# The end of a fused layer pair rewritten in the 65 dimensions of the last state and 32 of the memory

## The chip, the cores and the metric

One core of one Trainium2 chip. The metric is the device time of one execution in microseconds (us), lower is better; several executions are timed and their median is taken. Engines: TensorE (PE, with its weight loads PEld), VectorE (DVE), ScalarE (ACT), GpSimd (POOL), SyncE (SP, which issues all the DMAs here).

## What is computed

Input `x` is 8 sequences of 256 tokens, 2048 tokens of 512 values, float32. Cut to what matters:

```python
# first half: x1 = x + LN(attn(LN(x)))
h = LN(x) @ Win.T + bin                        # 64 dimensions
for layer in range(4):
    y = sconv(silu(LN(h)))                     # diagonal complex recurrence along the 256 tokens
    h = h + y * scl
    h = h + silu(LN(h) @ W1.T + b1) @ W2.T + b2   # 64 -> 256 -> 64
x1 = x + LN(LN(h) @ Wout.T + bout)             # 64 -> 512
# second half: out = x1 + LN(ffn(LN(x1)))
xn = LN(x1)
q = xn @ Wq.T                                  # 64 dimensions
scores = (q @ Wr.T) @ (keys @ Wr.T).T / sqrt(48) + log_rel     # 128 slots
top 8 of the scores; attn = q @ keys.T / sqrt(64) + log_rel over those 8; w = softmax
aux = (w @ values) @ Wvd.T @ Wvu.T             # 32 dimensions between
u = f(var(xn), mean over all tokens of log1p(var), gelu(xn @ Wu1.T + bu1) @ Wu2.T)
gate = sigmoid(...), zero below 0.05
out = x1 + LN(xn + gate * aux)
```

## The kernel before

The 2048 tokens are 16 tiles of 128 (TILES), in 4 groups of 4 tiles (GROUPS, GT). A unit u is one group in one layer, so there are 16 units. Every engine has its instructions written out by hand, in its own order, and waits on semaphores.

**Setup and start.** SP issues all input loads in one row: weights, then for each group the transposed input `XT` and `X` (1 MB each). PE's `first_h` (L1031) multiplies a group of `XT` by the input weights into the group's own PSUM bank (banks 2 to 5), where the state h of the group stays through all layers. ACT's `input_squares` (L397) sums the squares of x for the input norm, POOL's `input_rstd` (L312) makes 1/sqrt of it, and DVE's `first_h` (L716) scales h. DVE builds the tables of the recurrence. `keep_busy` (L1043) has PE multiply ones by ones into an unused part of a bank: 10 times before `turn1(0)`, 6 times before `turn1(1)` and `turn1(2)`.

**The steps.** 20 steps (STEPS, `step` on each engine) form a pipeline in which a unit passes: square on ACT (`square`, L449), sum on DVE (`sum_squares`, L729), power -0.5 on POOL (`norm`, L328), scaling on DVE (`scale_twice`, L735), transposes on PE (`turn1`, L1057), silu on ACT (`silu1`, L454), multiplication, scan and multiplication on DVE (L751, L760, L766), `mix_in` on PE (L1070), a second norm, `turn2` (L1082), `z_out` on ACT, `hidden` on PE (L1095), two silus on ACT (L476) and one step later `project` on PE (L1104, L1110). In step s, PE does turn1(s), project(s-3), turn2(s-2), mix_in(s-1), hidden(s-2), and in steps 4 to 9 one piece of `setup_late` (L1006), which multiplies the weights of the end together. In the same step ACT does square(s+1) after silu1(s); the unit s+1 is ready for it once project(s-3) is done. DVE does `score_rows` (L697) in step 6. PE's, ACT's and DVE's queues are in order: what is behind a wait stands.

**The first half's end.** Steps 16 to 19 hand over the last normed state as `ZL` (64 rows and a row of ones). For every tile PE multiplies it by `WO`, 512 wide (`output`, L1140); ACT squares and sums it (L505), POOL makes 1/sqrt (`pair_rstd`, L340), DVE adds it to X (`first_result`, L809), takes statistics (L814), POOL makes the next 1/sqrt, DVE normalises into `XN` (L822).

**The second half.** PE transposes XN in four pieces (`turn_xn`, L1151), ACT copies them out (L510), and PE makes 384 columns in four pieces of 128 rows each (`scores`, L1164): 128 routing scores, 128 attention scores, 128 inputs of the gelu. ACT does the gelu (L516); DVE finds the top 8 and masks the others (`select_pair`, L830), and takes the largest (`pair_max`). These run two pairs behind `output` on the same engines. Then the gate is worked out in small steps on DVE, ACT takes exponentials of a pair (`exps`, L535), PE transposes them (`turn_e`, L1195), ACT copies them out (`e_out`, L540), PE multiplies by the 512-wide `V2` (`memory`, L1207), DVE adds the result to XN (`mix`, L966), ACT sums the squares (L546), POOL makes 1/sqrt, and DVE (12 tiles, `finish`, L972) or POOL (4 tiles, L370 and L373) writes the output tile; SP stores a pair of tiles at a time (L282).

## Time and profile before

| | |
|---|---|
| median of 3 runs | 251.32 us (251.24 to 251.65) |
| the profiled execution | 250.35 us |
| its span, first to last instruction | 248.5 us |
| PE busy | 196.7 us, 79% |
| DVE busy | 181.2 us, 73% |
| ACT busy | 128.3 us, 52% |
| POOL busy | 89.4 us, 36% |
| mean granted clock of PE | 0.952 of full speed |

The first `turn1` starts at 21.89 us, that of step 16 at 126.89, that of step 19 at 141.91; the last output tile is finished at 245.3. A busy share is an average over stages with different limits; the rows below are therefore taken by stage. A matmul of float32 shows as two records, a transpose as one. The records of a run of matmuls overlap, so the pace of a run is its length over its records.

### The profile page before, as it was taken

The numbers are of one execution on the slowest core, as the hardware profiler recorded it, in microseconds if no ns is written. First come the engines' busy times: TensorE is split into PE (matmuls) and PEld (weight loads), VectorE is DVE, ScalarE is ACT, GpSimd is POOL, SyncE is SP. The second block draws the span as 40 slices with busy tenths as digits, with TensorE's granted clock in tenths as the row PEclk, the third lists the DMA queues.
The fourth block names the chain that finished last, engine by engine and source line by source line (L and its number), as shares of the span: only waits on it lengthen the run. The fifth ranks groups of instructions, "written<-read, shape, count | busy, mean of one in ns | idle before, by whom it ended". The sixth has DMA issues, their size and how long they took to land.

```text
span 248.5 us, 3501 instructions
## 1 busy us (share of the span) xinstructions
PE 196.7 (79%) x1148; PEld 145.2 (58%) x1148; DVE 181.2 (73%) x507; ACT 128.3 (52%) x306; POOL 89.4 (36%) x118
## 2 busy tenths in 40 slices
PE   2699596389959998878888759999999999399600
PEld 2699495377848787767776525565556555143200
DVE  7799895557784777767663174977797775889993
ACT  4328728246543667575565644343243329587640
POOL 8213333433342443533334332121212110048772
PEclk9999989799997999999999999999999999979965
DMA  5999900000000000000000000000000000003346
GB/s 197 425 415 419 258 9 4 0 0 1 3 0 0 3 0 0 4 0 0 3 0 3 0 0 1 1 3 0 0 0 0 0 3 1 0 0 120 135 169 253
DMA packets 5407, 15.09 MB, mean 61 GB/s; under 512 B 909, under 2 KB 1773, under 8 KB 4366
## 3 DMA queue, kind: packets, MB, share of 16 engines
q1 hardware_dynamic: 5390, 14.88, 16.2%
q8 instruction: 9, 0.15, 0.2%
q14 instruction: 8, 0.07, 0.1%
HBM read 10.68 MB, written 4.19 MB: 60 GB/s over the span
## 4 chain that ended last, share of the span: by engine, by line
PE 49%; DVE 25%; POOL 10%; ACT 9%; issue 4%; POOLq 0%; DVEq 0%; ACTq 0%
PE bank L1164 15%; PE bank L1110 12%; POOL RS L328 8%; PE bank L1140 5%; PE bank L1057 4%; DVE Z L735 3%; DVE SS L729 3%; PE bank L1207 3%; PE bank L1070 2%; ACT SQ L449 2%; PE bank L1151 2%; DVE XT L966 2%; DVE X L972 2%; PE bank L1038 2%; PE bank L1095 1%
## 5 line engine op out<-in xcount | busy, mean ns | idle before, releaser
L328 POOL TENSOR_TENSOR RS<-SS,nhalf 128x4 f32<-128x4 f32 x36 | 43.1, 1209 | 72.0 <-DVE SS L729 71.8
L1164 PE MATMUL bank<-SW_,Y 128*128 128x384 f32 x128 | 43.9, 485 | 0.0
L729 DVE TENSOR_REDUCE SS<-SQ 128x4 f32<-128x260 f32 x36 | 15.1, 423 | 26.1 <-ACT SQ L449 25.0
L1164 PEld LDWEIGHTS bank<-SW_,Y 128*128 128x128 f32 x128 | 23.9, 190 | 17.0 <-issue 4.2
L1110 PE MATMUL bank<-ffst,HD 128*128 128x128 f32 x256 | 33.5, 287 | 0.0
L1110 PEld LDWEIGHTS bank<-ffst,HD 128*128 128x128 f32 x256 | 32.4, 205 | 0.3
L449 ACT ACTIVATE SQ<-bank 128x256 f32<-128x256 f32 x36 | 13.8, 383 | 29.4 <-PE bank L1110 18.1
L476 ACT ACTIVATE HD<-bank,b1r 128x512 f32<-128x512 f32 x32 | 20.3, 684 | 12.1 <-PE bank L1095 12.1
L1057 PE MATMUL bank<-ident,Z 128*128 128x128 f32 x64 | 11.5, 306 | 18.0 <-DVE Z L735 17.9
L1057 PEld LDWEIGHTS bank<-ident,Z 128*128 128x128 f32 x64 | 7.3, 151 | 23.7 <-DVE Z L735 23.7
L809 DVE SCALAR_TENSOR_TENSOR X<-bank,OR,X 128x512 f32<-128x512 f32 x16 | 11.3, 746 | 12.3 <-POOL OR L346 12.2
L760 DVE TENSOR_TENSOR_SCAN V<-cvst,U 128x514 f32<-128x514 f32 x16 | 19.5, 1219 | 0.0
L1095 PE MATMUL bank<-Z,w1r 64*128 64x256 f32 x128 | 18.1, 402 | 1.6 <-ACT Z L470 1.6
L1038 PE MATMUL bank<-wcc,XT 128*128 128x128 f32 x128 | 17.3, 300 | 2.2 <-DVE wcc L633 2.2
L516 ACT ACTIVATE V<-bank 128x128 f32<-128x128 f32 x16 | 4.3, 277 | 28.4 <-PE bank L1164 28.4
L1038 PEld LDWEIGHTS bank<-wcc,XT 128*128 128x128 f32 x128 | 16.9, 217 | 2.5 <-issue 2.4
L1070 PE MATMUL bank<-cvst,U 128*128 128x128 f32 x128 | 17.9, 285 | 0.1
L1140 PE MATMUL bank<-WO,ZL 128*128 128x512 f32 x32 | 16.2, 597 | 1.6 <-DVE X L809 1.6
L1207 PE MATMUL bank<-V,U 128*128 128x512 f32 x32 | 16.8, 649 | 0.8 <-ACT U L540 0.7
L454 ACT ACTIVATE Y<-bank,cvst 128x512 f32<-128x512 f32 x16 | 12.4, 777 | 9.6 <-PE bank L1057 9.6
L1070 PEld LDWEIGHTS bank<-cvst,U 128*128 128x128 f32 x128 | 16.4, 201 | 0.3 <-DVE U L766 0.3
L735 DVE TENSOR_TENSOR Z<-bank,RS 128x512 f32<-128x512 f32 x16 | 11.1, 691 | 7.0 <-POOL RS L328 6.9
(219 smaller groups left out, 376.1 us busy)
## 6 DMA issues: line engine op xcount, KB each, us to landing
XT<-in_xT SPq DMA_DIRECT2D x4, 1024.0 KB, 11.4
X<-in_x SPq DMA_DIRECT2D x4, 1024.0 KB, 14.1
out<-X SPq DMA_DIRECT2D x8, 512.0 KB, 2.8
w1r<-in_w1d SPq DMA_DIRECT2D x1, 516.0 KB, 11.6
lt<-in_late SPq DMA_DIRECT2D x1, 385.5 KB, 19.3
w2r<-in_w2n SPq DMA_DIRECT2D x1, 256.0 KB, 7.1
SW_<-in_wu SPq DMA_DIRECT2D x1, 256.0 KB
c<-in_c SPq DMA_DIRECT2D x1, 172.5 KB, 21.8
```

Of the source, the lines that this page charges most:

```text
L328: pool.tensor_tensor(RS[:, g, :], SS[:, g, :], nhalf[:, :], ALU.pow).then_inc(done, 1)
L476: act.activation(HD[:, u % 2, a, :].rearrange("p (h n) -> p h n", h=2), FB[a], ACT.Silu, bias=b1r[:, 2 * L + a:2 * L + a + 1]).then_inc(g2, 1)
L729: dve.tensor_reduce(SS[:, g, :], SQ[:, g, :, :], AX.X, ALU.add).then_inc(done, 1)
L760: dve.tensor_tensor_scan(V[:, g, :], cvst[:, L, DC0:DC0 + UC], U[:, g, :], 0.0, ALU.mult, ALU.add).then_inc(v1, 1)
L1038: last = pe.matmul(HK[g][:, j * P:(j + 1) * P], XT[:, g, c, j * P:(j + 1) * P], wcc[:, c, :], start=(j == 0 and c == 0), stop=(c == VC - 1 ...
L1057: last = pe.transpose(T1B[:, j * P:(j + 1) * P], Z[:, g, j * P:(j + 1) * P], ident[:, :])
L1070: last = pe.matmul(HK[g][:, j * P:(j + 1) * P], U[:, g, j * P:(j + 1) * P], cvst[:, L, MX0:MX0 + P], start=False, stop=True, skip_group_ch ...
L1095: last = pe.matmul(FB[a][:, h, :], w1r[h * DIM:(h + 1) * DIM, L * DFF + a * P:L * DFF + (a + 1) * P], Z2[h * DIM:(h + 1) * DIM, g, :], sta ...
L1110: last = pe.matmul(HK[g][:, j * P:(j + 1) * P], HD[:, u % 2, a, at:at + P], ffst[:, L, a * P:(a + 1) * P], start=False, stop=True, skip_gr ...
L1140: pe.matmul(OB[t % 2][:, :], ZL[:, t // GT, (t % GT) * P:(t % GT + 1) * P], WO[:, :], start=True, stop=True).then_inc(o_mm, 1)
L1164: last = pe.matmul(SBK[t % 4][:, 0:SW], XNT[:, t % 4, c * P:(c + 1) * P], SW_[:, c, :], start=False, stop=(c == VC - 1))
L1207: pe.matmul(MB[t % 4][:, :], ET[:, t // 2 % 2, (t % 2) * P:(t % 2 + 1) * P], V2[:, :], start=True, stop=True).then_inc(aux_mm, 1)
```

## The change

1. x is multiplied, tile by tile, by a stacked matrix M of 289 columns (65 of the output weights with their bias, 128 of Wu1, 64 of Wq, 32 of Wvu), centred over its 512 rows. `project_x` on PE: four pieces of 128 rows, into bank 1, which `turn2` uses too; `x_out` on ACT copies the 289 columns out. Tiles are placed in steps by `XSTEP`.
2. At the start four small matmuls (`mix_columns`) and four of 289 columns (`column_sums`) stand on PE before `first_h(1)`; ACT copies both out before its step 0; POOL centres M (`centre_m`). `first_h(3)` moves from step 1 to step 0. `keep_busy` goes. M is loaded before the second group's XT.
3. The last state stays token-major in `F`, and transposed in `ZL`. The variance of the 512-wide result comes from a Gram matrix: `gram` on PE (four matmuls of 65 columns) and DVE, `cross` on POOL, `rho` and `first_rstd` on POOL.
4. `mixed` on PE (224 columns, 65 rows deep, one per tile) and `project` on DVE add the state's part to x's part; `unscore` on DVE, `scaled` and `gelu` on ACT, `turn_q` on PE, `qt_out` on ACT follow, and `scores` has 256 columns and 64 rows of depth.
5. In the last loop the memory is 32 wide (`memory`, two matmuls of 64 columns), `dots` on DVE and a chain of some ten small operations on POOL give the last norm, `factors` on DVE writes the factors into F, and one 512-wide matmul a tile (`output`) with one DVE operation (`finish`) makes the output tile. POOL no longer writes output tiles.
6. `setup_late` has five other pieces, in steps 4 to 8; `score_rows` is 256 wide (before: 384); `output_sums` and `setup_last` go.

The core of the diff:

```diff
+        XSTEP = {1: (0, 1), 2: (2, 3), 3: (4,), 9: (5,), 11: (6,), 13: (7,), 15: (8,), 16: (9,), 17: (10, 11),
+                 18: (12, 13), 19: (14, 15)}
+        SELS = PAIRS
+        BATCHES = ((0, 4), (4, 8), (8, 12), (12, 14), (14, 16))
+        LAST = [e // 2 - 1 for _, e in BATCHES]
+        MIXLAG = 3
+        FIN = {4: (0,), 5: (1,), 6: (2,), 7: (3,), 8: (4,), 9: (5, 6), 10: (7,)}
...
 ACT
+            def x_out(t):
+                act.wait_ge(xa_mm, t + 1)
+                act.activation(XA[:, t, :], LB[:, 0:MW], ACT.Copy).then_inc(xa_read, 1)
...
                 if 0 <= s - LATE0 < LATES:
                     setup_late(s - LATE0)
+                for t in XSTEP.get(s, ()):
+                    x_out(t)
...
+            for k in range(SELS + MIXLAG):
+                if k < SELS:
+                    exps(k)
                     e_out(k)
+                    y_out(k)
+                if k == 1:
+                    act.wait_ge(sig_in, 1)
...
+                for p in FIN.get(k, ()):
+                    f_out(p)
...
 DVE
+                g = s - UNITS - 1
+                if g >= 1:
+                    first_variance(g - 1)
+                if g >= 0:
+                    gram(g)
+                if g >= 1:
+                    project(g - 1)
...
+            def project(p):
+                for t in (2 * p, 2 * p + 1):
+                    dve.wait_ge(am_mm, 2 * p + 2)
...
+            def finish(t):
+                dve.wait_ge(o_mm, t + 1)
+                dve.scalar_tensor_tensor(out=X[:, t, :], in0=X[:, t, :], scalar=GX[:, 4, t:t + 1], in1=OB[t % 2][:, :],
+                                         op0=ALU.mult, op1=ALU.add).then_inc(out_ready, 1)
...
+            for k in range(SELS + MIXLAG):
+                if k < SELS:
+                    select(k)
+                for i in range(len(BATCHES)):
+                    if LAST[i] + MIXLAG == k:
+                        factors(i)
+                if k == 0:
+                    for p in range(5):
+                        learned(p)
+                if k == 1:
+                    for p in range(5, PAIRS):
+                        learned(p)
+                    gate_learned()
                     gate_sum()
+                if k == 2:
                     gate_mean()
+                    gate_level()
+                if 0 <= k - 1 < SELS:
+                    dots(k - 1)
+                if k == 2:
+                    gate()
+                for p in FIN.get(k, ()):
+                    finish(2 * p)
+                    finish(2 * p + 1)
...
 PE
+            def project_x(t, s):
+                pe.wait_ge(m_done, VC)
+                pe.wait_ge(cs_read, 1)
+                if t >= 1:
+                    pe.wait_ge(xa_read, t)
...
+                for c in range(VC):
+                    last = pe.matmul(LB[:, 0:MW], XT[:, g, c, j * P:(j + 1) * P], M[:, c, :], start=(c == 0),
+                                     stop=(c == VC - 1))
...
-                if u < 3:
-                    keep_busy(10 if u == 0 else 6)
...
-                if s + 2 < GROUPS:
-                    first_h(s + 2)
+                if s == 0:
+                    first_h(2)
+                    first_h(3)
                 if ffn:
                     hidden(s - 2)
                 if 0 <= s - LATE0 < LATES:
                     setup_late(s - LATE0)
+                for t in XSTEP.get(s, ()):
+                    project_x(t, s)
...
+            for s in range(STEPS):
                 step(s)
+                if s >= UNITS:
+                    gram(s - UNITS)
+                if s >= UNITS + 2:
+                    mixed(s - UNITS - 2)
...
+            mixed(2)
+            for p in range(PAIRS):
+                if p + 3 < PAIRS:
+                    mixed(p + 3)
+                turn_q(p)
+            scores(0)
+            scores(1)
+            for k in range(SELS + MIXLAG):
+                if k < SELS:
                     turn_e(k)
+                    memory(k)
+                    if k + 2 < SELS:
+                        scores(k + 2)
+                if k == 1:
+                    mean_sum()
+                for p in FIN.get(k, ()):
+                    turn_f(p, min(k + 1, SELS))
+                    output(2 * p)
+                    output(2 * p + 1)
```

`turn_e(k)` waits for the exponentials of pair k (`exps(k)` on ACT), which wait for `select(k)` on DVE. `turn_f(p, n)` transposes F of two tiles into the bank that `turn_e` uses, and waits for the n-th `e_out` and for `factors`; `f_out` on ACT copies it out. `mixed(p)` for odd p waits until `project(p-1)` is done.

## Rows read from the trace of the kernel before

**Rows 1.** Busy time by stage: PE, PEld, DVE, ACT, POOL (instructions), clock, DMA share, GB/s.
```profile
139.20:211.30 72.10, 67.23 (x253) 38.93 (x251) 51.08 (x180) 32.13 (x80) 15.85 (x33) 1.00 0.00 1
211.30:245.30 34.00, 18.29 (x44) 7.19 (x44) 31.49 (x70) 19.39 (x68) 18.83 (x24) 0.85 0.28 104
245.30:248.50 3.20, 0.00 (x0) 0.00 (x0) 0.03 (x1) 0.00 (x0) 0.00 (x0) 0.50 0.56 210
```

**Rows 2.** Chain that ended last: start, us, what.
```profile
98.38 0.66 PE bank L1057 x4
...
126.89 0.63 PE bank L1059 x4
...
131.89 0.63 PE bank L1059 x4
...
174.40 2.58 PE bank L1164 x8
```

**Rows 3.** Timeline of step 11 and the start of step 12: start, us, engine, line.
```profile
98.98 1.95 PE L1110 MATMUL bank<-ffst,HD 128*128 128x128 f32 x16
...
101.97 1.13 PE L1095 MATMUL bank<-Z,w1r 64*128 64x256 f32 x8
...
104.05 0.66 PE L1057 MATMUL bank<-ident,Z 128*128 128x128 f32 x4 [0.95 <-DVE Z L735]
```

**Rows 4.** Timeline, steps 2 and 3.
```profile
34.95 0.38 ACT L449 ACTIVATE SQ<-bank 128x256 f32<-128x256 f32 x1 [1.18 <-DVE bank L722]
...
44.17 0.38 ACT L449 ACTIVATE SQ<-bank 128x256 f32<-128x256 f32 x1
...
47.73 1.12 PE L1057 MATMUL bank<-ident,Z 128*128 128x128 f32 x4 [4.76 <-DVE Z L735]
```

**Rows 5.** Timeline, step 7, behind the pause that score_rows leaves.
```profile
74.01 0.70 PE L1057 MATMUL bank<-ident,Z 128*128 128x128 f32 x4 [2.80 <-DVE Z L735]
...
74.72 3.47 PE L1110 MATMUL bank<-ffst,HD 128*128 128x128 f32 x16
```

**Rows 6.** Timeline, from the last selects to the memory's matmuls.
```profile
207.25 0.49 DVE L834 MAX8 M<-bank 128x8 f32<-128x128 f32 x2
...
209.57 0.42 DVE L854 TENSOR_REDUCE NMX<-cvst 128x2 f32<-128x256 f32 x1
...
214.22 0.17 DVE L908 TENSOR_SCALAR GA<-GA 128x16 f32<-128x16 f32 x1
...
215.87 0.17 DVE L916 TENSOR_SCALAR GA<-GA 128x16 f32<-128x16 f32 x1
...
216.20 0.39 ACT L535 ACTIVATE U<-cvst,NMX 128x128 f32<-128x128 f32 x1
...
217.11 0.44 PE L1195 MATMUL bank<-ident,U 128*128 128x128 f32 x2 [3.44 <-ACT U L535]
...
217.59 0.38 ACT L540 ACTIVATE U<-bank 128x256 f32<-128x256 f32 x1 [0.53 <-PE bank L1195]
...
223.11 1.88 PE L1207 MATMUL bank<-V,U 128*128 128x512 f32 x4
```

**Rows 7.** Lines: what, shape, count, busy us, mean ns, idle before.
```profile
L809 DVE SCALAR_TENSOR_TENSOR X<-bank,OR,X 128x512 f32<-128x512 f32 x16 | 11.3, 746 | 12.3 <-POOL OR L346 12.2
L972 DVE SCALAR_TENSOR_TENSOR X<-XT,ZR,X 128x512 f32<-128x512 f32 x12 | 11.2, 970 | 0.6 <-POOL ZR L346 0.6
L827 DVE SCALAR_TENSOR_TENSOR V<-V,lt 128x128 f32<-128x128 f32 x16 | 3.9, 282 | 0.0
L743 DVE TENSOR_TENSOR Z<-bank,RS 128x256 f32<-128x256 f32 x20 | 8.1, 407 | 3.3 <-POOL RS L328 3.3
```

**Rows 8.** Windows of a microsecond, columns as in rows 1.
```profile
215.00:216.00 1.00, 0.00 (x0) 0.00 (x0) 0.86 (x5) 0.00 (x0) 0.00 (x0) 1.00 0.00 0
...
218.00:219.00 1.00, 1.00 (x2) 0.46 (x2) 0.97 (x4) 0.79 (x3) 0.00 (x0) 0.50 0.00 0
...
221.00:222.00 1.00, 1.00 (x3) 0.42 (x3) 0.97 (x3) 0.98 (x4) 0.92 (x2) 0.87 0.00 0
```

More of the change, by code:

```diff
@@ new lines, in _ @@
+            for s in range(STEPS):
+                if s == 0:
+                    mix_rows()
+                    column_means()
+                step(s)
+                if s == 0:
+                    ffn_out()
+            for p in range(PAIRS):
+                scaled(2 * p)
+                scaled(2 * p + 1)
+                gelu(p)
+                if p >= 1:
+                    qt_out(p - 1)
+            qt_out(PAIRS - 1)
+            act.wait_ge(ln_in, 1)
+            act.activation(GA[:, 3, :], GA[:, 2, :], ACT.Ln).then_inc(ln_out, 1)
@@ new lines, in _ @@
+            first_variance(2)
+            gram(3)
+            unscore(0)
+            project(2)
+            unscore(1)
+            project(3)
+            unscore(2)
+            project(4)
+            unscore(3)
+            first_variance(3)
+            project(5)
+            unscore(4)
+            gate_variance()
+            project(6)
+            unscore(5)
+            project(7)
+            unscore(6)
+            unscore(7)
+            for k in range(SELS + MIXLAG):
[11 more added lines that the diff above has]
+                    gate_learned()
@@ L1004, in setup_ffn, with mix_columns, column_sums @@
                 last.then_inc(w2_mm, 1)
+            def mix_columns():
+                pe.wait_ge(s_m, 32)
+                pe.wait_ge(lt_ready, 3)
+                for c in range(VC):
+                    last = pe.matmul(LB[:, c * ZD:(c + 1) * ZD], WOR[:, c * P:(c + 1) * P], LT[:, :], start=True,
+                                     stop=True)
+                last.then_inc(bp_mm, 1)
+            def column_sums():
+                pe.wait_ge(bp_read, 1)
+                for c in range(VC):
+                    last = pe.matmul(LB[:, 0:MW], ones[:, :], M[:, c, :], start=(c == 0), stop=(c == VC - 1))
+                last.then_inc(cs_mm, 1)
@@ L1013, in setup_late @@
+                vals = ltc("vals").rearrange("p (c n) -> p c n", c=VC)
+                wvd = ltc("wvd").rearrange("p (c n) -> p c n", c=VC)
+                if i == 0:
+                    for c in range(VC):
+                        last = pe.matmul(LB[0:VB, NSLOT:2 * NSLOT], wvd[:, c, :], vals[:, c, :], start=(c == 0),
+                                         stop=(c == VC - 1))
                 if i == 1:
-                    pe.wait_ge(s_late, 48)
-                    vals = ltc("vals").rearrange("p (c n) -> p c n", c=VC)
@@ L1029, in setup_late @@
+                    last = pe.matmul(LB[:, NSLOT:NSLOT + VB], vpT[:, :], G2[:, :], start=True, stop=True)
+                if i == 4:
+                    pe.wait_ge(mf_done, 1)
+                    for c in range(VC):
+                        last = pe.transpose(LB[:, c * P:(c + 1) * P], MF[:, c, :], ident[:, :])
                 last.then_inc(late_mm, 1)
@@ L1041, in first_h @@
                 last.then_inc(h0_mm, 1)
-            def keep_busy(n):
-                for _ in range(n):
-                    pe.matmul(T2B[:, HW:HW + P], ones[:, :], ones[:, :], start=True, stop=True)
             def turn1(u):
                 g = u % GROUPS
-                if u < 3:
-                    keep_busy(10 if u == 0 else 6)
                 pe.wait_ge(z1, u + 1)
@@ new lines, in gram, with mixed @@
+            def gram(g):
+                if g == 0:
+                    pe.wait_ge(zm_eps, 1)
+                pe.wait_ge(y1, UNITS + g + 1)
+                pe.wait_ge(z1, UNITS + g + 1)
+                for j in range(GT):
+                    last = pe.matmul(GB[g][:, j * ZD:(j + 1) * ZD], ZL[:, g, j * P:(j + 1) * P], ZM[:, 0:ZD], start=True,
+                                     stop=True)
+                last.then_inc(gr_mm, 1)
+            def mixed(p):
+                g = p // 2
+                pe.wait_ge(gr_prod, g + 1)
+                if p % 2:
+                    pe.wait_ge(t_done, 2 * p)
+                for t in (2 * p, 2 * p + 1):
+                    pe.matmul(AB[g][:, t % 2, 0:AW], ZL[:, g, (t % GT) * P:(t % GT + 1) * P], ZM[:, ZD:MW], start=True,
+                              stop=True).then_inc(am_mm, 1)
@@ new lines, in turn_f, with output @@
+            def turn_f(k, after):
+                i = min(i for i in range(len(BATCHES)) if 2 * k + 2 <= BATCHES[i][1])
+                pe.wait_ge(f_done, i + 1)
+                pe.wait_ge(et_ready, after)
+                if k >= 1:
+                    pe.wait_ge(ft_ready, k)
+                for j in range(2):
+                    last = pe.transpose(EB[:, j * P:(j + 1) * P], F[:, 2 * k + j, :], ident[:, :])
+                last.then_inc(f_tr, 1)
+            def output(t):
+                pe.wait_ge(ft_ready, t // 2 + 1)
+                if t >= 2:
+                    pe.wait_ge(out_ready, t - 1)
+                else:
+                    pe.wait_ge(qt_done, PAIRS)
+                    pe.wait_ge(gsum_read, 1)
+                pe.matmul(OB[t % 2][:, :], FT[:, t // 2 % 2, (t % 2) * P:(t % 2 + 1) * P], FM[:, :], start=True,
+                          stop=True).then_inc(o_mm, 1)
```

726 lines of the change are left out of this document (369 added, 357 removed).

## The prediction, written before the changed kernel was run

> **What bounds the kernel now.** I read the busy times by stage first, then the chain that ended last, then timelines of single steps. Three stages have three limits. In the end of the first half and the scoring (139.2 to 211.3 us) PE is busy 67 of 72 us [rows 1]; the chain there is matmul behind matmul, with 2.58 us for the 384 columns of each tile [rows 2]. From 211.3 to 245.3 DVE is busy 31.5 of 34 us [rows 1]. Before them, a step (from 98.38 to 104.05, 5.67 us [rows 2, 3]) is bound by a loop: transposes and `project` on PE, square, sum, power and scaling on the other engines. PE is done with `hidden` at 103.10 and waits 0.95 us for the scaled group [rows 3]. So PE has about one free microsecond a step, and none in the end. The change takes PE and DVE work out of the end and puts a part of it into the steps.
>
> **What goes.** From turn1(16) at 126.89 [rows 2] to the end at 248.5 are 121.6 us; this stretch is replaced whole, so I lay out the new one and don't subtract.
>
> **The price of `project_x`.** 8 records of 384 columns take 2.58 us, so 8 of 289 columns take 2.58 x 289/384 = 1.94 us at the high clock. The copy `x_out` has 289 columns, a little over the 256 of `e_out`, 0.38 [rows 6]; I take 0.42. Bank 1 is single, so two tiles in one step cost 2 x 1.94 + 0.5.
>
> **Start: +7.8.** The extra matmuls before `first_h(1)` (1.94 for the column sums, about 0.6 for the small ones) push square(1) back by about 1.5, which `first_h(3)`, now earlier, gives back. Then comes the term that counts. In steps 1 and 2 `x_out` stands at the end of ACT's step, ahead of square(2) and square(3). PE starts tile 0 after mix_in(0), near 33.6; tile 1 is copied out near 38.8, so square(2), before at 34.95 [rows 4], starts there. In step 2 the same again: turn1(2) near 42, mix_in and `hidden` to 46, tiles 2 and 3 to 51.1. square(3), before at 44.17 [rows 4], comes at 51.1: +6.9. Sum, power and turn1(3) follow it as before, so turn1(3) moves from 47.73 [rows 4] to 54.6. Tile 4 in step 3 takes 1.94 of PE against 1.0 free: +0.9. Bounds of this part: +4 if PE's short waits stay at the high clock and the copies overlap, +9 if not.
>
> **Steps 4 to 8: -1.9.** The new `setup_late` pieces are about as long as the old, +0.3. `score_rows` has 256 columns for 384, -0.5. And step 6 now has 1.94 us of matmuls (289 columns, four pieces) in the pause in which PE waited 2.80 us; behind that pause 16 records took 3.47 us [rows 5] in place of 1.95 [rows 3], at half clock. I take the pause as filled and the fall as gone, -1.7; bound 0.
>
> **Steps 9 to 15: +4.0.** Four tiles, one in a step, each 1.94 + 0.1 against 0.95 free [rows 3]: +1.1 each. `setup_last`, which delayed step 13, goes: -0.4. turn1(16) so comes at 126.9 + 7.8 - 1.9 + 4.0 = 136.8.
>
> **Steps 16 to 18: 26.2.** Step 16 is bound by PE: 4.65 of old work, 1.94, and `gram` (four matmuls of 65 columns, near 0.7): 7.3. Step 17 (4.5 of old work, two tiles 4.4, gram 0.6): 9.6. Step 18: 2.3 + 4.4 + 0.6 + `mixed` 0.75 = 8.0, and then `project(0)` on DVE (two of 224 columns, by 407 ns for 256 [rows 7]) stands ahead of the scaling that turn1(19) needs: 9.3. turn1(19) at 163.0; before 15.0 after turn1(16).
>
> **To the first select: 20.** PE reaches `mixed(1)` 6.2 us into step 19. Behind it DVE has 7 pairs of `project` (0.7), 8 of `unscore` (0.5), a gram product and sum (1.15), two variances (1.2), `gate_variance` (1.9) and short waits for `mixed` (0.7): 19 to 20. First select at 183.0.
>
> **Turns 0 to 3 of the last loop: 18.5, bound by DVE.** A select took 2.74 from 207.25 to 209.99 [rows 6], with two `learned` (0.28 long, a little over 0.2 apart [rows 7]) and one mask operation (about as long) that go: 2.05. Four of them 8.2; 8 pairs of `learned` 3.6; the gate's small operations at 0.21 each (8 from 214.22 to 216.04 [rows 6]) 4.1 in all; three `dots` at 0.7; 0.6 of waits. Turn 4 starts at 201.5.
>
> **Turns 4 to 7: 33.2, bound by a chain.** Here is the step that decides. In PE's queue turn_f, and with it the output matmuls, stand behind `turn_e(k)`, which waits for the exponentials of pair k, which wait for select(k); and in DVE's queue `finish` stands ahead of select(k+1). So nothing of turn k+1 overlaps turn k. Its length: select 2.05; exponentials 0.05 + 0.86 (216.20 to 217.06); turn_e 0.05 + 0.44; e_out 0.04 + 0.38 [rows 6]; memory 0.4; scores, bias rows and two 64-row matmuls of 256 columns, 0.8; turn_f 0.45; f_out 0.43; two output matmuls 0.1 + 1.88 [rows 6]; the last `finish` 0.05 + 0.75 [rows 7]. Sum 8.7; without scores in turns 6 and 7, 7.9. Two of each: 33.2. DVE works 4.8 of each.
>
> `finish` replaces L972, mean 970 ns, but reads PSUM as L809 does, mean 746 ns [rows 7]; I take 0.75, since the operands are L809's. The Trainium skill (GPSIMD Engine Reference, the table of its specifications) says that GpSimd contends with VectorE instructions with two SBUF inputs. `finish` has one, so by it 0.75 holds even beside GpSimd; at L972's 0.97 the sum would be about 1.5 us longer, as only the last of a pair is on the path.
>
> **Turns 8 to 10: 14.1, and 3.2 behind.** Turn 8 is factors, turn_f, f_out, two outputs, finish: 4.5. The last three pairs overlap on PE and DVE: 9.6. From the last finish to the end 3.2, as now [rows 1]. At the high clock the sum is 201.5 + 33.2 + 14.1 + 3.2 = 252.0.
>
> **The clock: +5.** When PE stood idle for 3.4 us up to 217.11 [rows 6], the granted clock was still 1.00 in the window from 215, fell to 0.50 as work came back, and rose in the window from 221 [rows 8]: from 2.4 to 1.2 GHz for almost 4 us. In each of turns 4 to 7 PE stands 3.8 us (0.8 + 2.05 + 0.96). I let turn_e, memory, scores and turn_f run at half clock: +1.35 with scores, +1.1 without, 5 in all. Bounds: 0, or +3.5 a turn if the outputs run slow too, 14. The Trainium skill (TensorE: Matmul & The Clock Gate, the section on the HAM clock gate) says that the ramp costs under 1% of a typical span. That would be under 2.5 us here and give a span of at most 254.5; step 7 alone lost 1.5 [rows 3, 5], so I keep 5.
>
> **Sum.** Span 257.0. The profiled execution took 1.85 us more than its span (250.35 for 248.5), so 258.9, against 250.35: +8.5. The median of the runs lies 1.0 above the profiled execution, inside the error of this sum. I forecast 259.
>
> **The rivals.**
> Slower, high clock kept in turns 4 to 7: 252.0 + 1.9 = 253.9. For it: the memory stage kept 0.85 of the clock though PE was busy 18 of 34 us [rows 1]; against: pauses of 4.76, 2.80 and 3.44 us each ended in slow records [rows 4, 5, 8]. Chance 0.2.
> Slower, low clock throughout the last loop: +9 on the forecast at most, some 266. Chance 0.1.
> Faster: the last loop is bound by DVE, not by the chain. Place: turns 4 to 7. If they took DVE's 4.8 each, 33.2 would become 19 and the clock term go: 252.0 - 14 + 1.9 = 240. It decides against me as soon as a turn takes under 7.8 us with the slow clock counted (8.5 us in four turns). For it: DVE filled 31.5 of 34 us in the same place before [rows 1]; against: the order of the queues. Together with a start at its lower bound this is the faster side. Chance 0.26.
> No change: the 41 us (16 x 2.58 [rows 2]) of PE's scoring and what is added cancel; a band of 1 us in a spread of 20. Chance 0.04.
> The forecast itself: 0.4.
>
> Faster, same and slower mean more or less than 0.2%, about what a measurement of this kernel can tell from no change: 0.26, 0.04, 0.70. The range leaves out a tenth on either side: 243 holds most of the faster case, 267 the low clock.
>
> **What would show it.** turn1(3) near 54.6 with ACT's square(3) behind `x_out`, turn1(16) near 137, turn1(19) near 163, first select near 183. In turns 4 to 7 starts of select 8 to 10 us apart, DVE idle ahead of `finish` for PE, the clock falling in each. Wrong if selects are 5 us apart, or if turn1(16) comes before 132.

## The result and the profile after

The changed kernel takes 281.93 us (median of 4 runs, 279.75 to 282.54) against 251.45 (251.24 to 251.65) for the kernel before: ratio 1.1197, interval 1.1133 to 1.126, **slower by 12%**. The forecast was 259, from 243 to 267: right in the sign, wrong by 23 us in the size. The profiled execution took 279.75 us with a span of 277.9. Executions of one and the same kernel lie some microseconds apart, the longer ones with the lower granted clock (the changed kernel from 279.75 us at 0.840 to 282.54 at 0.824, e7_start_lag_gatevar below from 244.88 at 0.909 to 251.28 at 0.876), so medians are compared with medians, and lengths of stages are read from the profiled executions.

The place of each term of the sum, forecast and found (starts in us of the span; the length in brackets where that is what was forecast):

| place | forecast | found | miss of the term |
|---|---|---|---|
| turn1(3) | 54.6 | 55.34 | |
| turn1(16) | 136.8 | 138.85 | +2.05 |
| turn1(19) | 163.0 (26.2 behind it) | 166.86 (28.0) | +1.8 |
| first select | 183.0 (20) | 195.24 (28.4) | +8.4 |
| turn 4 | 201.5 (18.5) | 213.79 (18.55) | 0 |
| end of turn 7 | 33.2, and 5 for the clock | 259.56 (45.8) | +7.6 |
| last finish ends | 14.1 | 274.66 (15.1) | +1.0 |
| span | 257.0 | 277.9 | +20.9 |

Two terms hold 16 of the 21 us. Busy time by stage, cut at those places (columns as in [rows 1]):

```profile
21.90:55.30 33.40, 23.02 (x134) 18.06 (x134) 20.69 (x48) 18.70 (x44) 12.77 (x12) 0.92 0.25 99
55.30:138.90 83.60, 79.44 (x590) 68.34 (x591) 56.49 (x100) 46.64 (x93) 31.15 (x28) 0.97 0.00 1
138.90:166.90 28.00, 24.66 (x161) 20.35 (x159) 7.21 (x20) 9.22 (x19) 8.96 (x10) 1.00 0.00 1
166.90:195.20 28.30, 19.45 (x71) 14.09 (x72) 15.02 (x51) 12.92 (x37) 7.73 (x12) 0.67 0.00 0
195.20:213.80 18.60, 12.17 (x46) 6.58 (x44) 15.36 (x96) 6.61 (x26) 1.69 (x6) 0.50 0.01 1
213.80:259.60 45.80, 29.62 (x72) 13.70 (x72) 16.25 (x62) 8.44 (x33) 9.58 (x39) 0.59 0.09 35
259.60:277.90 18.30, 10.64 (x24) 4.02 (x24) 7.67 (x17) 1.53 (x4) 2.56 (x11) 0.91 0.39 145
```

In the fourth and sixth no engine is full: PE 19.45 of 28.3 and 29.62 of 45.8, VectorE 15 and 16. Such a stage is bound by a chain that passes from engine to engine. The stage that I took for VectorE's and that mostly was (the fifth, 15.36 of 18.6) came out as forecast, in part by luck, as told further down.

The same cut for the whole of the replaced part, before and after, is the case in two lines. The kernel before, from its turn1(16), then the changed kernel from its own:

```profile
126.90:248.50 121.60, 96.39 (x385) 55.69 (x385) 87.13 (x258) 58.83 (x160) 38.15 (x61) 0.94 0.09 35
```
```profile
138.90:277.90 139.00, 96.55 (x370) 58.73 (x368) 61.52 (x243) 38.73 (x116) 30.51 (x77) 0.72 0.08 31
```

The change took 25.6 us of work from VectorE and 20.1 from ScalarE, and the part is 17.4 us longer. PE is busy as long as before, with fewer columns: its clock is 0.72 where it was 0.94. The other 12 us are the later turn1(16), 138.85 for 126.89.

The page: engines, clock in 40 slices, the chain by engine. In [rows 8] the clock was low for a few us; here it is under 8 tenths in thirteen slices from the last projections to the turns of the last loop.

```profile
PE 214.8 (77%) x1196; PEld 160.1 (58%) x1196; DVE 156.5 (56%) x495; ACT 112.6 (41%) x276; POOL 82.7 (30%) x140
...
PEclk9999997869999999999999999655555555766799
...
PE 60%; DVE 14%; DMA 7%; ACT 5%; issue 5%; POOL 4%; SPq 3%; DVEq 0%; ACTq 0%
```

**Steps 2 and 3** (timeline, answers to [rows 4]): square(3), L541, at 51.80 stands behind the second copy of the projection, L492; turn1(3) waits 3.89 us and its four matmuls, slow, take 1.11.

```profile
49.26 2.19 PE L1168 MATMUL bank<-M,XT 128*128 128x289 f32 x8 [0.59 <-ACT XA L492]
51.49 0.41 ACT L492 ACTIVATE XA<-bank 128x289 f32<-128x289 f32 x1 [2.37 <-PE bank L1168]
51.80 0.38 ACT L541 ACTIVATE SQ<-bank 128x256 f32<-128x256 f32 x1
...
55.34 1.11 PE L1220 MATMUL bank<-ident,Z 128*128 128x128 f32 x4 [3.89 <-DVE Z L819]
```

**Two steps in the middle** (PE's timeline, answers to [rows 3]): the one with a tile takes 6.72 us, without a wait for the scaled group, the next, without a tile, 5.62 with 0.94 of wait. Forecast: 1.1 more; found: 1.1.

```profile
95.12 0.66 PE L1220 MATMUL bank<-ident,Z 128*128 128x128 f32 x4 [0.36 <-DVE Z L819]
...
101.84 0.60 PE L1220 MATMUL bank<-ident,Z 128*128 128x128 f32 x4
...
107.46 0.66 PE L1220 MATMUL bank<-ident,Z 128*128 128x128 f32 x4 [0.94 <-DVE Z L819]
```

**Ahead of the first select** (timeline; L1316 is `mixed` on PE, L929 `project` on VectorE): they take turns. PE stands for VectorE 3.01, 0.78 and 2.62 us, VectorE for PE 1.50, 0.38, 1.03, 1.49 and, for the first scores, 2.70. The four records of a pair take 1.83 us, at half clock, where `mixed(0)` took 0.97 at the high clock.

```profile
177.77 1.83 PE L1316 MATMUL bank<-ZM,Y 65*128 65x224 f32 x4 [3.01 <-DVE XT L929]
...
179.64 0.81 DVE L929 SCALAR_TENSOR_TENSOR XT<-bank,RHO,XA 128x224 f32<-128x224 f32 x2 [1.50 <-PE bank L1316]
...
181.35 0.81 DVE L929 SCALAR_TENSOR_TENSOR XT<-bank,RHO,XA 128x224 f32<-128x224 f32 x2 [0.38 <-PE bank L1316]
...
184.18 0.81 DVE L929 SCALAR_TENSOR_TENSOR XT<-bank,RHO,XA 128x224 f32<-128x224 f32 x2 [1.03 <-PE bank L1316]
...
188.68 1.83 PE L1316 MATMUL bank<-ZM,Y 65*128 65x224 f32 x4 [2.62 <-DVE XT L929]
190.54 0.81 DVE L929 SCALAR_TENSOR_TENSOR XT<-bank,RHO,XA 128x224 f32<-128x224 f32 x2 [1.49 <-PE bank L1316]
...
195.24 0.50 DVE L956 MAX8 M<-bank 128x8 f32<-128x128 f32 x2 [2.70 <-PE bank L1338]
```

**Turn 5** (timeline, 227.54 to 239.24, answers to [rows 6]): the closed loop that was forecast. ScalarE waits 6.43 us for the select, PE 3.52 for ScalarE, VectorE 7.51 for PE. Each of PE's groups is slow: the two outputs (four records), L1389, take 3.22 us for 1.88 in [rows 6]. `turn_e(5)` starts 2.82 us behind its select; in turn 4, the first line here, it starts 4.32 us behind (select at 213.79), because PE still had the matmuls of turn 3 to do.

```profile
218.11 0.69 PE L1358 MATMUL bank<-ident,U 128*128 128x128 f32 x2
...
229.43 0.40 ACT L616 ACTIVATE U<-cvst,NMX 128x128 f32<-128x128 f32 x1 [6.43 <-DVE NMX L969]
...
230.36 0.69 PE L1358 MATMUL bank<-ident,U 128*128 128x128 f32 x2 [3.52 <-ACT U L616]
...
235.31 3.22 PE L1389 MATMUL bank<-FM,V 128*128 128x512 f32 x4 [0.47 <-ACT V L634]
237.43 0.75 DVE L1079 SCALAR_TENSOR_TENSOR X<-X,GX,bank 128x512 f32<-128x512 f32 x1 [7.51 <-PE bank L1389]
```

**Lines** (answer to [rows 7], columns the same): `finish`, L1079, lasts 747 ns, as forecast, and stands behind 36 us of idle time. The Trainium skill (GPSIMD Engine Reference, the table of its specifications) names contention with GpSimd for VectorE instructions with two SBUF inputs, and `finish` has one. The trace agrees: all sixteen last 746 to 749 ns, the one at 262.57 too, beside which GpSimd was computing by the timeline.

```profile
L1389 PE MATMUL bank<-FM,V 128*128 128x512 f32 x32 | 23.0, 858 | 3.8 <-ACT V L634 3.8
L1079 DVE SCALAR_TENSOR_TENSOR X<-X,GX,bank 128x512 f32<-128x512 f32 x16 | 12.0, 747 | 36.1 <-PE bank L1389 35.7
L1316 PE MATMUL bank<-ZM,Y 65*128 65x224 f32 x32 | 11.6, 511 | 6.4 <-DVE XT L929 6.4
```

**The clock** (windows of a microsecond, answers to [rows 8]): it falls during the pause of 3.01 us that ended at 177.77, and is back at 1.00 only with the last outputs of turn 5. In turns 6 and 7 it falls again, to a mean of 0.66 and 0.67.

```profile
175.00:176.00 1.00, 0.00 (x0) 0.00 (x0) 0.93 (x4) 0.00 (x0) 0.61 (x1) 1.00 0.00 0
176.00:177.00 1.00, 0.00 (x0) 0.00 (x0) 1.00 (x4) 0.06 (x1) 0.93 (x2) 0.70 0.00 0
177.00:178.00 1.00, 0.23 (x1) 0.26 (x2) 1.00 (x4) 0.83 (x3) 0.51 (x1) 0.50 0.02 8
...
237.00:238.00 1.00, 1.00 (x3) 0.34 (x1) 0.57 (x1) 0.00 (x0) 0.00 (x0) 0.58 0.00 0
238.00:239.00 1.00, 0.54 (x2) 0.00 (x0) 0.60 (x2) 0.00 (x0) 0.00 (x0) 1.00 0.00 0
```

### The profile page after: what moved, and what is told of

The parts are those of the page before. It is cut to its first block, busy times and chain, and to the rows that moved or that the text cites. A ratio compares the mean times of both kernels' runs of the same rounds, so it can differ in the third digit from the quotient of the medians.

```text
span 277.9 us, 3663 instructions
## 1 busy us (share of the span) xinstructions
PE 214.8 (77%) x1196; PEld 160.1 (58%) x1196; DVE 156.5 (56%) x495; ACT 112.6 (41%) x276; POOL 82.7 (30%) x140
## 3 DMA queue, kind: packets, MB, share of 16 engines
q1 hardware_dynamic: 5486, 14.94, 14.1%
## 4 chain that ended last, share of the span: by engine, by line
PE 60%; DVE 14%; DMA 7%; ACT 5%; issue 5%; POOL 4%; SPq 3%; DVEq 0%; ACTq 0%
PE bank L1168 12%; PE bank L1274 11%; PE bank L1389 8%; DMA XT<-in_xT 7%; PE bank L1259 4%; PE bank L1232 4%; POOL RS L354 4%; PE bank L1316 3%; PE bank L1220 3%; PE bank L1368 3%; PE bank L1338 2%; DVE Z L819 2%; PE bank L1208 1%; PE bank L1379 1%; DVE tmpA L962 1%
## 5 line engine op out<-in xcount | busy, mean ns | idle before, releaser
L1168 PE MATMUL bank<-M,XT 128*128 128x289 f32 x128 | 35.3, 417 | 3.3 <-ACT XA L492 3.3
L1079 DVE SCALAR_TENSOR_TENSOR X<-X,GX,bank 128x512 f32<-128x512 f32 x16 | 12.0, 747 | 36.1 <-PE bank L1389 35.7
L1274 PEld LDWEIGHTS bank<-ffst,HD 128*128 128x128 f32 x256 | 31.5, 201 | 0.2
L1168 PEld LDWEIGHTS bank<-M,XT 128*128 128x128 f32 x128 | 23.2, 191 | 13.6 <-issue 8.4
L1389 PE MATMUL bank<-FM,V 128*128 128x512 f32 x32 | 23.0, 858 | 3.8 <-ACT V L634 3.8
L541 ACT ACTIVATE SQ<-bank 128x256 f32<-128x256 f32 x36 | 13.8, 383 | 24.7 <-PE bank L1274 19.5
L1259 PE MATMUL bank<-Z,w1r 64*128 64x256 f32 x128 | 19.1, 419 | 0.7 <-ACT Z L559 0.7
L441 POOL TENSOR_TENSOR GX<-RES,GA 128x4 f32<-128x4 f32 (+1 forms) x5 | 1.0, 197 | 55.0 <-DVE XQ L1065 35.2
L1316 PE MATMUL bank<-ZM,Y 65*128 65x224 f32 x32 | 11.6, 511 | 6.4 <-DVE XT L929 6.4
L1358 PE MATMUL bank<-ident,U 128*128 128x128 f32 x16 | 5.5, 447 | 14.0 <-ACT U L616 14.0
L492 ACT ACTIVATE XA<-bank 128x289 f32<-128x289 f32 x16 | 6.6, 412 | 23.9 <-PE bank L1168 23.9
```

Source lines behind the costliest of these rows:

```text
L1168: last = pe.matmul(LB[:, 0:MW], XT[:, g, c, j * P:(j + 1) * P], M[:, c, :], start=(c == 0), stop=(c == VC - 1))
L1259: last = pe.matmul(FB[a][:, h, :], w1r[h * DIM:(h + 1) * DIM, L * DFF + a * P:L * DFF + (a + 1) * P], Z2[h * DIM:(h + 1) * DIM, g, :], sta ...
L1274: last = pe.matmul(HK[g][:, j * P:(j + 1) * P], HD[:, u % 2, a, at:at + P], ffst[:, L, a * P:(a + 1) * P], start=False, stop=True, skip_gr ...
L1316: pe.matmul(AB[g][:, t % 2, 0:AW], ZL[:, g, (t % GT) * P:(t % GT + 1) * P], ZM[:, ZD:MW], start=True, stop=True).then_inc(am_mm, 1)
L1389: pe.matmul(OB[t % 2][:, :], FT[:, t // 2 % 2, (t % 2) * P:(t % 2 + 1) * P], FM[:, :], start=True, stop=True).then_inc(o_mm, 1)
```

## The experiments

Eleven kernels, all built from the changed one. In the first group (e1 to e4) the kernel before took 251.1 us (249.12 to 252.76), in the second (e5 to e8) 250.43 (249.83 to 252.20, and one execution of 684.82), in the third 249.99. The ratios are to it; differences to the changed kernel are taken from its 281.93.

**e1_fill: the clock by itself.** Matmuls of a matrix of ones into an unread part of bank 0 stand in PE's waits.

```diff
+            def keep_busy(n):
+                for _ in range(n):
+                    pe.matmul(EB[:, 3 * P:4 * P], ones[:, :], ones[:, :], start=True, stop=True)
...
                 if k < SELS:
+                    keep_busy((6, 2, 2, 8, 4, 12, 12, 12)[k])
                     turn_e(k)
```

> The changed kernel with dummy matmuls (ones by ones, 128 columns, into an unused part of bank 0) in PE's pauses between step 19 and the end: 10, 3 and 10 before mixed(3), mixed(5), mixed(7), 5 before scores(0), 2 to 12 before each turn_e, 8 before memory(2). Theory C (the half clock that holds from 176.7 to 237.9 us is the cause of the time missing in my sum): the granted clock stays at 1.0, the first select comes some 7 us earlier after turn1(19) (28.4 to about 21), turns 4 to 7 fall from 11.4 to about 8.8 us each, together about -18, so about 264 us for 282. Theory Q (only the order of the queues makes the turns long): the clock may rise but the time falls by under 3 us. If the dummies themselves delay PE, the time rises.

Measured: 269.62 us (269.3 to 269.75), ratio 1.0753 (1.068 to 1.0826): 12.3 below the changed kernel, more than the theory of the queues allowed and less than that of the clock claimed. `mixed` and the outputs are faster, by lines:

```profile
L1389 PE MATMUL bank<-FM,V 128*128 128x512 f32 x32 | 17.7, 679 | 3.8 <-ACT V L634 3.8
L1079 DVE SCALAR_TENSOR_TENSOR X<-X,GX,bank 128x512 f32<-128x512 f32 x16 | 11.9, 747 | 27.9 <-PE bank L1389 27.1
L1316 PE MATMUL bank<-ZM,Y 65*128 65x224 f32 x32 | 7.4, 362 | 2.7 <-DVE XT L929 2.7
```

The starts of its selects 4 to 7 are 212.77, 226.61, 235.39 and 243.17. So turns 5, 6 and, from a finish that ends at 251.0, 7 take 8.8, 7.8 and 7.9 us where the changed kernel took 11.7, 10.1 and 10.2; the forecast for the high clock was 8.7, 7.9 and 7.9. The loop was sized right to 0.1 us, and the clock cost 7.6 us in three turns. Turn 4 is no test of it: the granted clock was 0.63 in it here too, and it takes 13.8 us as before. Of the 10.0 us of span, 1.0 lies ahead of the first filler. The stretch from turn1(19) to the first select is 27.0 us for 28.4, and this doesn't clear the clock there: VectorE's waits for `mixed` fell from 4.4 to 1.5 us, but the five fillers ahead of `scores(0)` ran at the low clock and stood in its way for 2.1 us.

```profile
189.43 2.34 PE L1399 MATMUL bank<-ones 128*128 128x128 f32 x10
```

**e2_lag: the closed loop opened.** The finish of a pair goes one turn back on VectorE, behind the next select.

```diff
-                for p in FIN.get(k, ()):
+                late = FIN.get(k - 1, ()) if k <= SELS else ()
+                now = FIN.get(k, ()) if k >= SELS else ()
+                for p in late + now:
                     finish(2 * p)
```

> The changed kernel with only DVE's order changed: the two finish operations of turn k stand behind select(k+1) and dots(k), so that the select and exponentials of the next pair run beside the output matmuls. Theory Q (a turn is one chain because finish stands ahead of the next select): turns 4 to 7 lose the 3 to 4 us of finish, select and exponentials that now run beside PE, from 11.4 to about 8.5 at the half clock; about -10, so 272 us. Theory C alone (PE's slow records set the pace): under 3 us are won, since PE's own records and hand-overs fill a turn.

Measured: 259.15 us (258.05 to 261.22), ratio 1.0347 (1.0262 to 1.0432): 22.8 below the changed kernel, twice what was expected. The selects of its timeline:

```profile
214.88 0.49 DVE L956 MAX8 M<-bank 128x8 f32<-128x128 f32 x2
219.31 0.49 DVE L956 MAX8 M<-bank 128x8 f32<-128x128 f32 x2 [0.71 <-PE bank L1340]
228.64 0.49 DVE L956 MAX8 M<-bank 128x8 f32<-128x128 f32 x2
...
233.88 0.49 DVE L956 MAX8 M<-bank 128x8 f32<-128x128 f32 x2
```

Turns 4, 5 and 6 take 4.4, 9.3 and 5.2 us for 13.8, 11.7 and 10.1. That is 16.5 us; the end comes 5.2 sooner behind select(7), and the start was 1.1 later in this execution: 20.6 of span. Turn 4 has no finish any more, and its outputs are paid for in turn 5, in which PE is busy 8.1 of 9.3 us. The clock is still 0.50 from 188 to 228, through turns 4 and 5, so that the gain in these two (11.7 of the 16.5) isn't clock. In turn 6 and behind it the clock is back, at 0.98 for 0.66, and shares in the gain.

**e3_fill_lag: both.**

> Both edits, with 3 dummies in place of 12 before turn_e in turns 5 to 7. If both theories hold, turns 4 to 7 come to 5.5 to 6.5 us each, -20 in all, and the first select -7: about 254 us. If the two are the same loss seen twice, the result is near the better of the two single edits.

Measured: 256.68 us (255.84 to 261.79), ratio 1.0228 (1.0143 to 1.0312): 2.5 below e2_lag. The clock is 0.96 for 0.872, and the fillers are worth 2.5 us net where they were worth 12.3. The two edits singly won 35.1 us and together 25.3, so in good part they win the same loss. What is left of the clock's price shows turn by turn: turns 4 and 5 take 3.0 and 6.8 us for 4.4 and 9.3, at a clock of 1.00 for 0.50. Against it, turns 0 to 3 are 1.4 us longer than in e2_lag and the part behind select(7) 2.0.

**e4_start: the order on ScalarE in steps 2 and 3.**

```diff
                 if s < GROUPS:
                     square(s, (h0_done, s + 1), sq1)
+                if s in (2, 3):
+                    x_out(2 * s - 4)
                 if s + 1 < GROUPS:
                     input_squares(s + 1)
+                if s in (2, 3):
+                    x_out(2 * s - 3)
...
-                for t in XSTEP.get(s, ()):
+                for t in XSTEP.get(s, ()) if s > 2 else ():
                     x_out(t)
```

> The changed kernel with only ACT's order changed in steps 1 to 3: the copies x_out(0) and x_out(1) stand behind square(2), with input_squares(3) between them, and x_out(2), x_out(3) behind square(3). If my start term is right (the copies stand ahead of the squares that the steps wait for, +6.9 us), square(3) moves from 51.8 to about 44 and the time falls by 6 to 8 us, to about 275. Rival: PE's matmuls themselves, 8 us in steps 1 and 2, are the price, and the order on ACT wins under 2 us.

Measured: 269.78 us (269.6 to 271.41), ratio 1.0782 (1.0688 to 1.0876): 12.1 below the changed kernel. In its timeline turn1(3) and turn1(4) start at

```profile
47.90 0.64 PE L1224 MATMUL bank<-ident,Z 128*128 128x128 f32 x4
...
54.61 0.60 PE L1224 MATMUL bank<-ident,Z 128*128 128x128 f32 x4
```

for 55.34 and 64.44. Of the 9.8 us, 7.4 are the order, what the forecast had for it (turn1(3) is where the kernel before has it, 47.73 in [rows 4]); 2.4 are step 3, 6.7 long for 9.1, whose matmuls no longer run behind a pause (clock 1.00 for 0.73 from 55 to 65). The rest of the kernel keeps its lengths: 28.4 to the first select, 53.8 from there to select(7) for 54.1.

**e5_start_lag: do they add?**

> The changed kernel with two orders altered: in steps 2 and 3 ScalarE squares the group before it copies out the two input projections, and VectorE takes the finish of a pair one turn later, behind the next select. Alone they took 12.1 and 22.8 us off 281.9. Theory: they act in different stages (start: the wait and the slow PE records behind it before turn1(3); end: turns 4 to 7 no longer one closed loop), so they add: 247, from 245 to 249, below the kernel before. Rival: the lag's gain was partly clock that returned early, and an end that comes 10 us earlier finds the same low clock: still additive, since the clock fell at the same place of the work in both; more than 2 us from 247 would say that the two share a cause.

Measured: 250.2 us (248.67 to 251.0), ratio 0.9984 (0.995 to 1.0018). The medians are 3.2 us short of adding, more than the 2 us that by my own words would mean a shared cause. But the changed kernel's median lies 2.2 us above its profiled execution, and subtracting both gains from it counts these 2.2 twice. The profiled executions add: 277.9 less 20.6 less 10.1 is 247.2 of span, and it is 246.8. So I take the two for separate causes. With them the changed kernel is level with the one before.

**e6_start_lag_banks: the alternation.**

```diff
+        PB = (0, 1, 0, 2, 1, 3, 0, 2)
...
-                    pe.matmul(AB[g][:, t % 2, 0:AW], ZL[...], ZM[:, ZD:MW], ...)
+                    pe.matmul(AB[PB[p]][:, t % 2, 0:AW], ZL[...], ZM[:, ZD:MW], ...)
```

with the waits that a bank's reader needs.

> As e5_start_lag, and the eight pairs of mixed projections use four banks in turn (0,1,0,2,1,3,0,2) instead of one bank for two pairs in a row, so that PE does not wait for VectorE's project of the pair before. Theory A (the 8.4 us by which the stretch from turn1(19) to the first select was longer than predicted is an alternation of PE and VectorE through one bank, VectorE idle 1.5 + 0.4 + 1.0 + 1.5 us for PE): 3 to 5 us below e5_start_lag. Theory B (that stretch is bound by what VectorE itself does, or by ScalarE's chain of scaling, gelu and copies behind the last project): under 1 us. Theory C (it is the low clock: mixed records 1.83 for 0.97 us): 0 here, since these records stay slow.

Measured: 247.2 us (243.63 to 248.44), ratio 0.9828 (0.974 to 0.9916): 3.0 below e5_start_lag, and 25.3 us from turn1(19) to the first select for 27.7. Behind `mixed(1)` VectorE's `project` waits for PE no more, by its timeline:

```profile
168.64 0.80 DVE L937 SCALAR_TENSOR_TENSOR XT<-bank,RHO,XA 128x224 f32<-128x224 f32 x2
169.88 0.80 DVE L937 SCALAR_TENSOR_TENSOR XT<-bank,RHO,XA 128x224 f32<-128x224 f32 x2
171.13 0.81 DVE L937 SCALAR_TENSOR_TENSOR XT<-bank,RHO,XA 128x224 f32<-128x224 f32 x2
```

Theory A's mechanism holds, with 2.3 us in that stretch, under its 3 to 5. The profiled execution as a whole is only 0.2 us of span below e5_start_lag, because its clock comes back a turn later: turn 6 takes 8.4 us for 5.2. The turn in e5_start_lag, then in this run:

```profile
217.00:222.20 5.20, 4.13 (x19) 2.11 (x19) 4.31 (x18) 1.83 (x8) 1.82 (x6) 1.00 0.27 101
```
```profile
214.70:223.10 8.40, 7.28 (x19) 3.44 (x19) 4.28 (x18) 1.88 (x8) 2.90 (x11) 0.55 0.16 62
```

The Trainium skill (Perfetto Trace Analysis, Optimizing Tensor Performance) asks for just this, groups of matmuls that rotate through banks so that the reading of one lies beside the next; the run agrees, with 2.3 us.

**e7_start_lag_gatevar: nine small operations moved.** `gate_variance()` goes from between `project(5)` and `project(6)` to behind `unscore(7)`.

> As e5_start_lag, and VectorE does gate_variance (nine small operations, 2.2 us) behind the last unscore, where it stood idle 2.7 us ahead of the first select, instead of between project(5) and project(6), where PE waited 2.6 us for project(6). Theory A (chain through the bank): 2 us below e5_start_lag, less up to 0.7 if ScalarE's logarithm and its table load now delay the first exponentials. Theory B (ScalarE's chain decides): under 0.5.

Measured: 248.38 us (244.88 to 251.28), ratio 0.9877 (0.9829 to 0.9925): 1.8 below e5_start_lag; 25.8 us to the first select for 27.7. The expected 2 us are met in the median and in the stretch (1.9): it is a chain on which VectorE's order counts. The profiled execution, 244.88 us, is the shortest of the ten, and the rest of its gain is no part of this.

**e8_start_lag_both: the pair turned with the exponentials.** In turns 4 to 7:

```diff
                     turn_e(k)
+                    for p in FIN.get(k, ()):
+                        turn_f(p, k)
                     memory(k)
```

with the finished pair in the other half of bank 0, and one wait of ScalarE for both.

> As e5_start_lag, and in turns 4 to 7 PE transposes the finished pair right behind turn_e, into the other half of the same bank, and ScalarE copies both out one behind the other, so that memory and scores run beside the second copy and the outputs find their operand ready. Theory: with the lag the turn is still a loop of PE and ScalarE (turn_e, copy, memory, scores, turn_f, copy, outputs, 5.2 to 6.2 us), and what it waits for turn_f's copy (1.0 us warm, 1.98 us at the low clock) goes, 0.4 us of turn_f added ahead of the first copy: 0.6 to 1 a turn, 2.5 to 4 us in all. Rival: VectorE's finish and select set the turn by now: 0 to 1.

Measured: 246.69 us (245.53 to 247.9), ratio 0.9855 (0.9792 to 0.9919): 3.5 below e5_start_lag, inside the expected 2.5 to 4. Turns 5 and 6 take 8.65 and 4.7 us for 9.3 and 5.2, and the end comes 2.1 us sooner behind select(7). Even opened, the end is a chain of PE and ScalarE.

**e9_orders: all of them.**

> All order changes together on the changed kernel: start and lag (250.2), the four banks in turn (-3.0 alone), gate_variance behind the last unscore (-1.8 alone), and the finished pair turned together with turn_e (-3.5 alone). Theory (each takes a wait out of a different place): 250.2 - 3.0 - 1.8 - 3.5 = 241.9, from 240.5 to 244; the first select 23 to 24 us after turn1(19). Rival (the four banks and gate_variance both shorten the same chain ahead of the first select, behind which ScalarE's chain of gelu and copies is next, late already): banks and gate_variance together give only 3.5, 243.2 to 245. Both are faster than the kernel before.

Measured: 238.23 us (238.08 to 239.01), ratio 0.9525 (0.9484 to 0.9565). Better than the sum of the parts by 3.7, and than the range forecast: the first select is 21.3 us behind turn1(19), 6.4 less than in e5_start_lag, where 2.3 and 1.9 were won singly, and turns 5 and 6 are 1.1 us shorter than in e8_start_lag_both. My rival, that both shorten one chain and don't add, was wrong the other way. Why they more than add no run shows by itself. It may be that with PE ahead VectorE's 2.2 us fall in a free place, and part is clock: 0.80 in the stretch for 0.71 in e5_start_lag.

**e10_orders_xstep: a tile in each step.**

```diff
-        XSTEP = {1: (0, 1), 2: (2, 3), 3: (4,), 9: (5,), 11: (6,), 13: (7,), 15: (8,), 16: (9,), 17: (10, 11),
-                 18: (12, 13), 19: (14, 15)}
+        XSTEP = {1: (0, 1), 2: (2, 3), 3: (4,), **{s: (s - 4,) for s in range(9, 20)}}
```

> As e9_orders, and the projections of tiles 5 to 15 stand one in each of steps 9 to 19, instead of four in the alternate steps 9 to 15, one in 16 and two in each of 17, 18, 19. Theory by the prediction's sizes: a tile in a step that waits for other engines costs 1.1 us (6.72 against 5.67 measured), in a step that PE fills 2.2. Three more of the first, three fewer of the second: -3.3, 2.5 to 3.5 below e9_orders. Rival: PE's pause in steps 17 to 19 is then as long as what it saves (VectorE's project(0) and scale_last stand in the way): 0 to 1.5.

Measured: 233.04 us (232.01 to 233.54), ratio 0.9297 (0.9249 to 0.9346): **7% faster than the kernel before, 17% faster than the changed kernel**, and 5.2 below e9_orders where 3.3 was expected. A tile in steps 10, 12 and 14 costs 1.0 us (turn1(16) 132.23 for 129.19), as sized. The second tile of a step that PE fills costs 2.9, not 2.2: step 17 takes 7.39 for 10.28, step 18 7.34 for 10.23, and the first select follows turn1(19) in 18.4 us for 21.3. PE must wait for the copy of the first tile (0.42 us and its way there and back) before it writes the second into the same bank. Stages from turn1(19) on:

```profile
155.00:173.00 18.00, 14.49 (x62) 10.33 (x60) 14.51 (x52) 12.22 (x37) 7.66 (x12) 0.73 0.00 0
173.00:191.40 18.40, 11.94 (x44) 6.53 (x42) 15.26 (x95) 6.37 (x24) 1.68 (x6) 0.50 0.01 1
191.40:214.00 22.60, 19.36 (x69) 10.57 (x70) 15.29 (x61) 7.77 (x34) 8.95 (x35) 0.71 0.13 50
214.00:231.80 17.80, 10.68 (x28) 4.14 (x26) 8.76 (x17) 1.68 (x5) 3.31 (x16) 1.00 0.46 174
```

The first is now 18.0 us with VectorE busy 14.5, near the forecast's 20, which had one more tile (2.9 us) in step 19. From select(4), at 191.40, to the end of the fourth pair's finish, at 216.44, it is 25.0 us, where the changed kernel took 45.8.

**e11_orders_fill: the clock once more.**

> As e10_orders_xstep, with matmuls of a matrix of ones in PE's waits ahead of the first scores and in each turn of the last loop (51 in all), which compute nothing. Theory (about 45 us of the last loop run at the granted clock of 0.5, and what is on PE's path there, some 4 us of a turn in turns 4 to 7, is stretched by it): clock over 0.95, 2 to 5 us below e10_orders_xstep. Rival: the fillers stand ahead of turn_e on the path and cost what they give, as between e2_lag and e3_fill_lag (-2.5): +1 to -1.

Measured: 232.29 us (232.03 to 234.01), ratio 0.9296 (0.9246 to 0.9346). The clock goes from 0.911 to 0.956 and the time from 233.04 to 232.29, inside the spread of both. The rival holds for the sum: fillers cost what they give. By place they don't. The profiled executions have 3.5 us more from turn1(19) to the first select (21.9 for 18.4), 1.7 of it in step 19 ahead of any filler and the rest behind it, and 2.7 us less in turn 5 (5.9 for 8.7), at a clock of 1.00 for 0.51. Fillers in the last loop alone weren't tried.

## Why the prediction was wrong, step by step

- **Start, +7.8: right in kind, 1.9 too short.** turn1(3) at 55.34 for 54.6, by the mechanism named; undoing it in e4_start gave 7.4 back. At turn1(4), where the term ends, it is 64.44 for 54.76 in the kernel before: +9.7, past my bound of +9. What was missing is the slow stretch behind the pause that it opens, 2.4 us: I let a pause be filled in step 7 and didn't ask which new one the change makes in step 3.
- **Steps 4 to 15: right.** Steps 4 to 8 gave -1.6 for -1.9, steps 9 to 15 +3.9 for +4.0, with 1.1 us for a tile, to a tenth. The 2.05 by which turn1(16) missed are the start's 1.9 and little else.
- **Steps 16 to 18, 26.2 for 28.0.** Right in kind, bound by PE, and 1.8 too short.
- **"To the first select: 20": the step that failed first and most, +8.4.** PE reached `mixed(1)` 6.2 us into step 19, as written. Behind it I added up VectorE's work and put "short waits for `mixed` (0.7)". The waits were 1.50 + 0.38 + 1.03 + 1.49, because one bank serves two pairs in a row, and 2.70 ahead of the scores, for ScalarE's chain behind the last project, which the sum hadn't at all: 7.1 for 0.7. The other 2.0 are the 1.0 until `mixed(1)` could be read and 1.0 more of VectorE's own work. e6 and e7 took 2.3 and 1.9 us out of it by order, at a clock that stayed low, e9 6.4 with both. What the low clock alone costs here stays open: e1 shows 1.3 net of 2.1 for its own fillers. It is the fault that the next step avoids: a sum of one engine's work is a lower bound, and the chain was there to be read from the waits in the code.
- **Turns 0 to 3, 18.5: right in the sum (18.55), in part by luck.** VectorE's work was some 2 us shorter than sized (a select 1.8 for 2.05, `dots` 0.5 for 0.7), and it stood 1.23 us for PE's `mean_sum` and 1.31 for an exponential of ScalarE, where I had 0.6 for all waits. The two misses cancel.
- **"Turns 4 to 7: 33.2, bound by a chain": right in kind and size, at the high clock.** e1 shows 8.8, 7.8 and 7.9 for 8.7, 7.9 and 7.9. Opening the loop by one line of order gave 20.6 us of span, 11.7 of them in turns 4 and 5 at the same low clock, so that it was the order of the queues that bound it, not work. Turn 4 took 13.8 for 8.7: in the changed kernel PE enters it with turn 3's transposes, memory and scores still to do (turn_e(3) at 214.32, when VectorE had begun select(4) at 213.79, and turn_e(4) at 218.11). turn_e stands 4.32 us behind its select there and 2.82 in turns 5 to 7, so this backlog, which a start "at 201.5" for all engines hid, is 1.5 us. The other 3.5 I put down to the clock, 0.50 throughout the turn; no run has this turn closed and at the high clock.
- **"The clock: +5": the second step that failed, the mechanism right, the size wrong.** It was about 11: 7.6 in turns 5 to 7 by e1, and the 3.5 of turn 4 by subtraction. I charged the parts ahead of the outputs, as if the clock came back with them in each turn. It was at 0.50 without a break from 177 to 237 us, the outputs of turn 5, and the outputs too ran slow: 2.3 to 2.9 us a turn in turns 5 to 7 for my 1.1 to 1.35, with the upper bound, "+3.5 a turn", nearer. The Trainium skill's rule that I set against it (TensorE: Matmul & The Clock Gate, the section on the HAM clock gate), under 1% of a span, is passed here by far: the clock cost about 11 us of 278 in turns 4 to 7 alone, and e1's fillers won 7.6 of them back in three turns.
- **The rivals.** The low clock throughout had a chance of 0.1 and a price of +9, "some 266"; it is nearest to what happened, though the clock alone explains only 6 of the miss. The forecast of 258.9, 6.1 more for the clock, 8.4 ahead of the first select, 1.5 of backlog, 2.05 up to turn1(16), 1.8 in steps 16 to 18 and 1.0 in turns 8 to 10 make the 279.75 that the profiled execution took. The faster rival, turns at VectorE's 4.8 us, was a statement on the order of the queues: e2 is that case in turns 4 and 6 (4.4 and 5.2 us, but 9.3 in turn 5), and the changed kernel isn't.
- **The range** was made of the bounds of single terms, with the stretch to the first select given none, since I had called it "19 to 20".
- **The price of the second tile** in steps 17 and 18: "two tiles 4.4" were 5.1 by e10 (2.2, and 2.9 with the wait for the copy), which is 1.4 of the 1.8.

Left open: what puts the return of the clock a turn later in one execution than in another. And no run took the change's parts apart by undoing the stacked projection itself; whether the memory's smaller dimension alone would pay wasn't tried.
